# One order behind the attention in place of another, and the full layer's first load issued earlier

## The reference

```
x = layernorm(x + block_attention(x))     # 16 heads of 8; a block of 64 queries sees 4 or 5 blocks
                                          # of keys, the first and last block of queries see all
h   = layernorm(x) * g + b ; a = softmax(q k / sqrt(8)) v @ wo     # full attention, 16 heads
x1  = x + a
hn2 = layernorm(x1) * g2 + b2
idx = argmax(hn2 @ gate_w + gate_b)       # one of 8 experts for each token
moe = relu(hn2 @ w1[idx] + b1[idx]) @ w2[idx] + b2[idx]            # 128 -> 512 -> 128
out = layernorm(x + (x1 + moe))
```

## Time and profile before

| | |
|---|---|
| median of 3 runs | 682.48 us (677.14 to 689.57) |
| profiled execution | 680.51 us, of which the span of instructions 678.7 |
| busy over the span | PE 88%, DVE 78%, ACT 70%, POOL 35% |
| mean granted TensorE clock | 0.942 of full |
| full layer's attention | about 231.5 to 582 us |
| sequence 0's tiles | about 586.5 to 630 us |
| sequence 1's tiles | about 630 to 665 us, the end to 678.7 |

### The profile page before, as it was taken

One profiled execution on the slowest core, in us unless ns is written; L12 is line 12 of the kernel. 1 busy time (PEld: TensorE's weight loads), 2 busy tenths in 40 slices (PEclk: granted clock), 3 DMA queues, 4 the chain that ended last, 5 costly groups with the idle time before them and its releaser, 6 DMA issues.

```text
span 678.7 us, 21729 instructions
## 1 busy us (share of the span) xinstructions
PE 597.3 (88%) x8674; PEld 292.1 (43%) x8674; DVE 530.0 (78%) x869; ACT 473.3 (70%) x997; POOL 239.9 (35%) x517
## 2 busy tenths in 40 slices
PE   4379999988899699989999999979999999789991
PEld 2244666665566453223233222322222222578891
DVE  3475668878467598998889999899999994188675
ACT  3016557766567558889888999868999989575650
POOL 9314531214767412281243315025110103227444
PEclk9555979999899899999999999999999999899997
DMA  3231222323111112211231222221122202738700
GB/s 100 29 47 24 31 31 43 51 35 45 27 27 28 27 27 57 57 25 37 46 56 24 44 49 48 41 40 23 27 36 39 57 17 76 214 114 234 223 22 12
DMA packets 32998, 37.14 MB, mean 55 GB/s; under 512 B 6200, under 2 KB 25185, under 8 KB 32898
## 3 DMA queue, kind: packets, MB, share of 16 engines
q1 hardware_dynamic: 31170, 32.59, 25.1%
q0 software_dynamic: 1728, 3.16, 1.3%
HBM read 15.65 MB, written 8.02 MB: 35 GB/s over the span
## 4 chain that ended last, share of the span: by engine, by line
PE 61%; DVE 17%; issue 9%; POOL 4%; DMA 4%; ACT 3%; SPq 1%; POOLq 0%; DVEq 0%; ACTq 0%
PE PO L1389 21%; PE RB L1428 20%; DVE NM L1176 12%; PE EX L1436 4%; PE EX L1247 3%; PE EX L1290 2%; DMA QKT<-QS 2%; PE EX L1361 2%; PE RB L1466 2%; POOL HN L776 1%; POOL sorted_rows L801 1%; PE EX L1276 1%; PE RB L1296 1%; ACT PR L915 1%; DVE ST L1090 1%
## 5 line engine op out<-in xcount | busy, mean ns | idle before, releaser
L1176 DVE TENSOR_REDUCE NM<-RB 128x1 f32<-128x1024 f32 (+2 forms) x416 | 422.8, 1063 | 81.8 <-PE RB L1428 70.3
L915 ACT ACTIVATE PR<-EX 128x512 f32<-128x512 f32 x736 | 390.7, 583 | 97.2 <-PE EX L1436 93.0
L1428 PE MATMUL RB<-QKT 48*64 48x128 bf16 (+4 forms) x1600 | 237.3, 311 | 30.7 <-DVE NM L1176 17.1
L1389 PE MATMUL PO<-PR,VB 128*32 128x128 f32 (+1 forms) x4160 | 248.6, 331 | 6.1 <-issue 4.9
L1436 PE MATMUL EX<-QKT 51*64 51x128 bf16 (+4 forms) x2048 | 238.3, 269 | 3.6 <-issue 1.9
L1389 PEld LDWEIGHTS PO<-PR,VB 128*32 128x32 f32 x4160 | 92.9, 110 | 118.8 <-ACT PR L915 73.4
L1428 PEld LDWEIGHTS RB<-QKT 48*64 48x64 bf16 (+1 forms) x1600 | 70.7, 108 | 161.9 <-DVE NM L1176 78.8
L1436 PEld LDWEIGHTS EX<-QKT 51*64 51x64 bf16 (+1 forms) x2048 | 83.1, 106 | 32.3 <-ACT PR L915 26.6
L840 POOL CAST MS<-NM 128x8 bf16<-128x8 f32 (+1 forms) x48 | 9.3, 193 | 246.8 <-DVE NM L1176 208.7
L829 POOL COPY VB<-VST 128x128 f32<-128x128 f32 (+1 forms) x64 | 18.6, 291 | 85.9 <-PE PO L1389 80.1
L881 ACT COPY XT<-EX 128x512 f32<-128x512 f32 x12 | 7.0, 586 | 32.3 <-PE EX L1276 31.2
(11 more groups left out here) (201 smaller groups left out, 538.5 us busy)
## 6 DMA issues: line engine op xcount, KB each, us to landing
QKT<-QS SPq DMA_DIRECT2D x64, 192.0 KB
QS<-in_L_ffn_w_dram SPq DMA_DIRECT2D x23, 256.0 KB, 3.3
sorted_rows<-ZERO SPq DMA_DIRECT2D x6, 514.0 KB, 9.8
PR<-in_L_ffn_w_dram SPq DMA_DIRECT2D x9, 256.0 KB, 3.8
TQ<-in_L_ffn_w_dram SPq DMA_DIRECT2D x6, 256.0 KB, 4.7
QKT<-MT SPq DMA_DIRECT2D x64, 3.0 KB
sorted_rows<-ZERO SPq DMA_DIRECT2D x2, 385.5 KB, 9.2
X<-_attn_hidden_states_dram SPq DMA_DIRECT2D x2, 384.0 KB, 4.0
```

The source lines that it names most:

```text
L915: nc.scalar.activation(PR[:, at % RING, h, 0:n], bank(key)[:, 0:n], ACT.Exp).then_inc(s_aread, 1)
L1176: nc.vector.tensor_reduce(NM[v % 2][:, h, tiles[0]:tiles[-1] + 1], ps, AX_X, ALU.max, negate=True).then_inc(s_dread, 1)
L1389: ins = pe.matmul(sums, VB[v % 2][:, L.kinds.index(kd), t, h, :], of, start=first and v % 2 == 0, stop=final and v % 2 == 1, skip_group_ch ...
L1428: ins = pe.matmul(spread(ps[r0:r1, c:c + of[1] * of[3]], of), columns(v, h, 0, ROWS6, (l0, 1, 0, ln)), columns(v, h, 1, ROWS6, of), start= ...
```

## The change

It has six parts. (1) `early` for units 0 and 16 goes from 3.0 to 9.6. The due time of unit 0's load stays at 16.0, its lower limit; that of unit 16 moves 6.6 ahead, which puts it before the row transfers of unit 14 in SP's list and behind the last `EXP` of unit 12 in PE's. (2) In `last_steps` `CT` and `WO` of sequence 1 come ahead of `XG` and `UP` of sequence 0. (3) `XG` of chunks 1 to 3 stands between `UP` 2 and `DN` 1, `UP` 6 and `DN` 5, `UP` 10 and `DN` 9, instead of right ahead of `UP` 4, 8 and 12. (4) `ARG` and the first two pairs of `SCALE` come one tile earlier (behind `UP` 3), `CNT`, the other two pairs, `SCAT` and `EJ` stay behind `UP` 4; `SCAT` waits for each tile's scaling on its own instead of for all. (5) For sequence 1 SP issues three weight loads, the first half of the sorted rows, two weight loads, the second half, and the rest, instead of eight weight loads ahead of all rows. (6) The last groups of normalization are 4, 2, 1 tiles instead of 3, 2, 2.

```diff
-NORM_GROUPS = ([(0, 4), (4, 8), (8, 12), (12, SB)], [(0, 4), (4, 8), (8, 11), (11, 13), (13, SB)])
+NORM_GROUPS = ([(0, 4), (4, 8), (8, 12), (12, SB)], [(0, 4), (4, 8), (8, 12), (12, 14), (14, SB)])
...
-ROUTED = 4
+ROUTED = 3
...
-    steps = [("XG", 0, 0), ("CT", 1, 0), ("CT", 1, 1), ("UP", 0, 0), ("WO", 1, 0), ("WO", 1, 1)]
+    steps = [("CT", 1, 0), ("CT", 1, 1), ("WO", 1, 0), ("WO", 1, 1), ("XG", 0, 0), ("UP", 0, 0)]
     steps += [("SUM", 1, (0, i)) for i in range(TT // 2)] + [("ROOT", 1, 0), ("SUMS", 1, 0), ("SUMS", 1, 1)]
     for n in range(1, SB + 1):
         if n < SB:
-            if n % 4 == 0:
-                steps.append(("XG", 0, n // 4))
             steps.append(("UP", 0, n))
         if n == ROUTED:
-            steps += [("ARG", 1, 0)] + [("SCALE", 1, (0, i)) for i in range(TT // 2)] + \
-                [("CNT", 1, 0), ("SCAT", 1, 0), ("EJ", 1, 0)]
+            steps += [("ARG", 1, 0)] + [("SCALE", 1, (0, i)) for i in range(2)]
+        if n == ROUTED + 1:
+            steps += [("CNT", 1, 0)] + [("SCALE", 1, (0, i)) for i in range(2, TT // 2)] + [("SCAT", 1, 0), ("EJ", 1, 0)]
+        if n % 4 == 2 and n + 2 < SB:
+            steps.append(("XG", 0, n // 4 + 1))
         steps.append(("DN", 0, n - 1))
...
-        early = 11.5 if v % UNITS else 3.0
+        early = 11.5 if v % UNITS else 9.6
...
-            for n in range(NW1):
-                load_first(1, n, W1S[1][n])
+            for n in range(3):
+                load_first(1, n, W1_PLACES[n])
             sp.wait_ge(s_scat[1], 16 * TT)
             wait_filled(sp, ("EXP", 1, UNITS - 1, LAST_EXP[1]))
-            load_sorted(1)
-            for n in range(NW1, SB):
-                if n < NW1 + NW0:
+            load_sorted(1, 0)
+            for n in range(3, 5):
+                load_first(1, n, W1_PLACES[n])
+            load_sorted(1, 1)
+            for n in range(5, SB):
+                if n >= NW1 + NW0:
+                    sp.wait_ge(s_h, n - NW1 - NW0 + 1)
+                elif n >= NW1:
                     wait_filled(sp, ("UP", 2, 0, n + 1))
-                else:
-                    sp.wait_ge(s_h, n - NW1 - NW0 + 1)
                 load_first(1, n, W1_PLACES[n])
...
-                    pool.wait_ge(s_norm, TT * (5 + u))
...
                     for g in range(u * TT, (u + 1) * TT):
+                        pool.wait_ge(s_norm, TT * 4 + g + 1)
```

More of the change, by code:

```diff
@@ L585, in load_first, with load_sorted @@
                 sp.dma_start(place, w1[bass.ds(e, 1), :, :].rearrange("o k f -> (o k) f")).then_inc(s_w1[b][n], 16)
-            def load_sorted(b):
+            def load_sorted(b, half):
                 r0 = b * SB
-                for i, (c0, c1) in enumerate(CHUNKS):
+                for i, (c0, c1) in list(enumerate(CHUNKS))[2 * half:2 * half + 2]:
                     sp.dma_start(XSB[b][:, c0:c1, :], XS[(r0 + c0) * P:(r0 + c1) * P, 0:HS]
@@ L652, in _ @@
             sp.wait_ge(s_scat[0], 16 * TT)
-            load_sorted(0)
+            load_sorted(0, 0)
+            load_sorted(0, 1)
             for n in range(NW0, SB):
```

## The result

Twenty runs of each kernel, taken in turns on the same chips: 683.69 us before (677.14 to 693.62), 670.66 us after (667.29 to 681.53). The ratio of the two is 0.9846 with a 95% interval of 0.9819 to 0.9873, which is 10.5 us of 683.69 (8.7 to 12.4). The ratio takes only executions within 1.5% of the fastest of their kernel, while the medians, which lie 13.0 apart, are of all of them. The profiled execution after took 669.51 us, 667.8 of them the span, against 680.51 and 678.7: 10.9 less in the span.

The account below looks back on a forecast made before the run. Three engines walk in step through the full layer's attention; what is winnable lies at its start and behind it. Gains 5.1 + 1.4 + 2.5 + 1.2 = 10.2 us give 670.3 profiled, 672 by the median, range 664 to 680.

Parts of the forecast that it names:

- Part 1: Start of full layer: earlier load of unit 16 removes PE's gap and the slow clock behind it; 5.1 us, 3.8 to 5.9.
- R3: Rival, 8%: unit 16's load does not really come earlier; its gain is 1 instead of 5.1 us, result 676.4.
- Part 2: Behind the attention: output products first bring DN 0 at 591.8 against 593.23; gain 1.4 us, none if the clock falls.
- R1: Rival, 23%: the clock falls again behind the attention, costing 1.4 us; result 673.7.
- the rule: Behind the attention: transposes do not hold the clock as products do, so it falls as before; 673.7 instead of 672.3.
- Parts 3 and 4: Sequence 0's tiles: columns ahead end three waits for ACT, 2.5 us; scalings by pairs shorten another, 1.2 us.
- R2: Rival, 13%: scalings still hold PE and columns find no room on ACT; result 674.5.
- Part 5: SP's loads for sequence 1: rows arrive before PE wants them, in new and old order alike; gain 0.
- R4: Rival, 3% with any other loss: SP's weights queue behind the wait for all scatters; slower, 684 at a landing of 632.
- Part 6: Last normalization groups at the kernel's end: longer wait for four tiles against a shorter last group; 0, -1.3 to +1.3 us.
- signs that the prediction names: New trace: DVE's addition under 3 us behind CTX, no column wait of UP, sequence 1's first scatter about 4.5 us earlier.

Follow-up runs that it names:

- gap_filled: Kernel before, plus 17 products of constants on PE during the wait for unit 16's load: 676.23 us against 687.66, ratio 0.9915.
- old_head: New kernel with the old order of the first six steps behind the attention: 673.76 us against before's 681.05, ratio 0.9868.
- output_behind_tiles: New kernel with XG and UP of sequence 0 between CT and WO: 673.31 us against before's 681.05, ratio 0.9832.
- load_alone: Kernel before with only the earlier load of unit 16 (early 9.6): 675.11 us against 687.66, ratio 0.989.
- old_groups: New kernel with the last normalization groups 3, 2, 2 again, on the slower chip: 701.04 us against before's 718.19, ratio 0.9864.
- weights_first: New kernel with SP's old order for sequence 1, eight weight loads before all rows, on the slower chip: 705.4 us against before's 718.19, ratio 0.9932.
- columns_late: New kernel with XG of chunks 1 to 3 back right ahead of the tile needing them: 672.72 us against before's 681.05, ratio 0.9852.
- scalings_at_once: New kernel with ARG and all eight scalings back behind UP 4: 670.0 us against before's 681.05, ratio 0.9796.

## Why the prediction was right, and where it was not

672 was predicted, 670.66 measured; 10.2 us of gain in the profiled execution against 10.9. That the medians agree so well is partly luck, as their distance of 13.0 us holds some 2.5 that the ratio (10.5 us) doesn't; the gain and its parts are the better test. By parts:

*Part 1*, 5.1 forecast. Measured 5.52 at the place and 5.67 at `CTX`. Both terms held: 4.3 for the gap (4.48, the rest of the 5.52), 0.8 for the clock (1.04, isolated by `gap_filled`). R3 is out: the load went out at 215.60, where 215.62 was worked out, and by the flight in `gap_filled` (220.73 to 229.60) it landed at 224.5, 2.6 us before PE was out of work.

*Part 2*, 1.4 forecast, 1.09 in the profiles, and this is the step that was wrong in kind. I priced the new order against the time that the old one had in the trace, and that time held a fall of the clock which came in two of four profiles with the old order. The prediction did say that the gain would be gone if the clock fell in the new order too; it did not ask what the old one takes without a fall. With the clock held the old order has 7.23 or 7.69 us to `DN` 0, 7.8 with the landing of before, and the new one 8.05, so the order by itself loses 0.2 to 0.8; against an old order whose clock fell it gains 0.6 (`old_head`) to 1.1 (before). The new order's own length was worked out well, 591.8 - 584.09 = 7.7 against 8.05; wrong was what it was taken from.

*R1 and the rule.* R1 didn't come true in the profile after: 1.00 in every microsecond from 578.8 to 589.8. It did come true on the disturbed chip, in all three profiles in which `CT` comes first; there the clock had been at half until about 2 us ahead of `CTX` too, and `DN` 0 came 9.44 and 9.49 behind `CTX` in the two with after's head: 1.4 over after, the price that R1 names. The Trainium skill's page "TensorE: Matmul & The Clock Gate", section "Part 4: PE-mode transpose", says that transposes do not count as busy time for the clock the way products do. `output_behind_tiles` agrees with it: with 1.75 us of transposes and no product for 4.14 us behind `CTX` the clock fell to half. After, with the first product 1.81 us behind `CTX`, it stayed. But `output_behind_tiles` doesn't show the rule, for PE also rested in it, 0.96, 1.05 and 0.87 us between the transposes, and rests alone could have done it. The rule doesn't tell the four runs of the old order apart either, in which PE rested 2.96 (before), 2.72 (`old_head`), 2.84 (`gap_filled`) and 2.38 us (`load_alone`) and the clock fell in the first two: in `old_head` it fell between 582 and 583, about 3.5 us behind the last sums (577.39 + 1.94), while `load_alone` and `gap_filled` had no product for 5.36 and 5.82 us and kept it. And 3.66 us without a product, from the last sums to the first output product, went at full clock after and ended at half in `old_groups` and `weights_first`.

*Parts 3 and 4*, 2.5 + 1.2 = 3.7 forecast, 4.20 measured. All four waits of the earlier trace rows are gone, as forecast. They were 0.87, 1.08, 0.87 and 0.76, 3.58 together, and PE's idle time in the stretch fell by 3.53 (from 3.92 to 0.39): the waiting that I left behind the scalings did not come. The other 0.67 is PE's busy time, 32.78 before and 32.11 after, a term that I did not have. It goes with the waits for columns, as it is 32.59 in `columns_late` and 32.12 in `scalings_at_once`; why is not shown. The split of the sum between the two parts has no single answer, as the undone halves show. R2 is out.

*Part 5*, 0 forecast, and no wait for rows was seen in any profile. Against R4 some 5 us were to spare: the first rows were issued 9.5 us ahead and took 3.9 to 4.3 to land.

*Part 6*, 0 forecast between -1.3 and 1.3, measured -0.04.

Of the signs that the prediction names, DVE's first addition is 3.04 us behind `CTX` and not under 3, and the first scatter 4.10 sooner against it, not 4.5. One wait of `UP` for its columns is left, 0.87 ahead of `UP` 0, where the new order itself puts it; the sum had 0.8 for these columns, but the list of signs says that there is none.

## What to carry to other kernels

Before an order is priced against the time in a trace, look at the clock of that stretch: a fall that may or may not come again is no part of what the old order costs, and the new one should be compared with it at the same clock, and with the same arrival of what it waits for. In a queue that waits in order, a load has a window and not only a latest place: 9.6 us ahead gained 5.5, and 16.0 lost 9.9 again, because what stood behind it was wanted first. When two edits take waits of the same engine away, undo each from the finished kernel and do each alone; their sizes differ by what they share, here 0.9 of 4.2 us. Spans of two halves that add up prove little by themselves: in `load_alone` 1.3 us lost in one stretch hid most of 1.9 gained in another.

## What the runs showed of the hardware

The clock behind the attention was not settled by the order of the instructions: with the same six steps it fell in two profiles and held in two. Nor was it settled by the length of PE's rest: it fell with 2.72 and 2.96 us and held with 2.38 and 2.84. What decides is open.

Half clock behind a gap of 4.4 us costs little, 1.04 us, and some 17 products of constants took it away.

One chip ran the kernel before in 718.19 us, where the others had 681 to 688, and each of the four profiles taken on it has PE standing still several times where the trace names nothing that could hold it for so long. PE in `old_groups`:

```profile
620.34 2.05 PE L1366 MATMUL EX<-QS 128*128 128x128 f32 x8 [5.77 <-issue]
...
627.77 2.07 PE L1252 MATMUL EX<-QS,XT 128*128 x8 [5.38 <-ACT X L945]
```

5.77 us of waiting for nothing that the profile shows and 5.38 for a copy of ACT that holds PE up for 1.08 us at most on the calm chips; the eight products behind each take 2.05 and 2.07 us, where eight took 1.06 to 1.16 after. Half clock lasted there even while PE worked: from 578 to 587 us PE is busy 9.00 of 9.00 us at a clock of 0.50. Where the stalls come from is open. Two of them together are longer than the whole gain of this change, and a ratio taken there says less than a distance between two stalls.
